# A two-layer graph network on one core: 93 of 3126 gathers of 128 rows replaced by single-row DMAs from SyncE and ScalarE

## The reference, cut to what matters

```python
h = x @ W
norm = dinv[src] * dinv[dst]
msgs = h[src] * norm[:, None]
out = jax.ops.segment_sum(msgs, dst, num_segments=n)
return out + b
```

## Time and profile before

| | us |
|---|---|
| median of 3 runs | 4136.05 |
| fastest, slowest run | 4133.31, 4149.07 |
| span of the profiled execution, first to last instruction | 4132.4 |
| POOL busy in it | 3025.7 |
| PE busy in it | 3066.6 |
| DVE, ACT busy in it | 1279.2, 392.7 |

### The profile page before, as it was taken

How to read it: one execution, slowest core, us unless ns; L and a number is a source line. 1 busy time by engine, 2 the same in 40 slices (tenths; PEclk the granted TensorE clock), 3 DMA queues, 4 the chain that set the end, 5 groups by cost and what they waited for, 6 DMA issues and landing times.

```text
span 4132.4 us, 36624 instructions
## 1 busy us (share of the span) xinstructions
PE 3066.6 (74%) x12107; PEld 1945.3 (47%) x12107; DVE 1279.2 (31%) x2593; ACT 392.7 (10%) x1088; POOL 3025.7 (73%) x3173
## 2 busy tenths in 40 slices
PE   6677777777776777777777777777778877777778
PEld 6344444443443443344444554444445555555556
DVE  8222222222222222222222233332224444434456
ACT  7000000000000000000001111111111111111112
POOL 3677777777777777777767777777777777777773
PEclk9878888888889888888879889999998899999988
DMA  8444444444444444444434444443334444444455
GB/s 268 135 118 118 118 119 119 118 119 120 119 118 119 118 121 118 119 119 118 121 100 119 119 118 121 118 118 112 113 113 120 117 118 118 115 121 129 118 153 176
DMA packets 248738, 513.99 MB, mean 124 GB/s; under 512 B 62491, under 2 KB 141832, under 8 KB 248296
## 3 DMA queue, kind: packets, MB, share of 16 engines
q0 software_dynamic: 150048, 410.73, 35.6%
q1 hardware_dynamic: 98504, 100.82, 8.2%
HBM read 471.70 MB, written 39.64 MB: 124 GB/s over the span
## 4 chain that ended last, share of the span: by engine, by line
POOL 66%; issue 22%; DMA 5%; PE 4%; DVE 1%; ACT 1%; SPq 0%; POOLq 0%; DVEq 0%
POOL sb_big L956 66%; DMA sb_big<-T,sb_srci 4%; PE bank L1241 2%; PE bank L570 1%; PE bank L1728 0%; ACT sb_big L791 0%; PE bank L1703 0%; PE bank L1713 0%; DVE sb_big L857 0%; DMA T<-sb_big 0%; PE bank L550 0%; DVE sb_big L859 0%; DMA sb_work<-dstT 0%; POOL sb_X L1900 0%; DVE sb_looks L668 0%
## 5 line engine op out<-in xcount | busy, mean ns | idle before, releaser
L956 POOL DMA_INDIRECT sb_big<-T,sb_srci x3126 | 2960.4, 947 | 975.9 <-issue 943.3
L1241 PE MATMUL bank<-sb_big 128*128 (+2 forms) x7056 | 2511.2, 463 | 987.8 <-DMA sb_big<-T,sb_srci 938.1
L1241 PEld LDWEIGHTS bank<-sb_big 128*128 128x128 f32 x7056 | 1303.3, 216 | 1954.6 <-issue 1816.3
L1001 DVE SCALAR_TENSOR_TENSOR sb_big<-sb_dstf,bank 128x2304 f32<-128x2304 f32 x196 | 499.0, 2546 | 29.9 <-issue 29.8
L1031 DVE SCALAR_TENSOR_TENSOR sb_work<-sb_bW,sb_work,bank 128x256 f32<-128x256 f32 x98 | 47.2, 481 | 1292.3 <-PE bank L1168 1292.3
L1016 DVE TENSOR_TENSOR sb_work<-bank,sb_work 128x257 f32<-128x257 f32 (+1 forms) x196 | 83.2, 425 | 461.3 <-PE bank L1241 461.3
L1040 DVE SCALAR_TENSOR_TENSOR sb_work<-bank,sb_dinv,sb_b 128x256 f32<-128x256 f32 x98 | 47.4, 484 | 529.3 <-PE bank L1168 529.3
L1070 ACT COPY sb_work<-bank 128x256 f32<-128x256 f32 x196 | 73.0, 373 | 1263.9 <-PE bank L1129 1263.9
L1050 DVE TENSOR_TENSOR sb_X<-sb_X,bank 128x256 f32<-128x256 f32 x98 | 41.2, 421 | 390.2 <-PE bank L1181 390.2
L1079 ACT ACTIVATE sb_work<-sb_work,sb_dinv 128x256 f32<-128x256 f32 x98 | 49.9, 509 | 878.4 <-DVE sb_work L1032 878.4
L1128 PE MATMUL bank<-sb_ident,sb_work 128*128 128x128 f32 x392 | 118.7, 303 | 16.9 <-DVE sb_work L1040 11.9
(11 more groups left out here) (200 smaller groups left out, 1719.7 us busy)
## 6 DMA issues: line engine op xcount, KB each, us to landing
sb_big<-T,sb_srci POOLq DMA_INDIRECT x3126, 2.8
sb_work<-T SPq DMA_DIRECT2D x49, 257.0 KB
T<-sb_work SPq DMA_DIRECT2D x49, 256.0 KB, 2.4
sb_work<-T SPq DMA_DIRECT2D x49, 256.0 KB
sb_X<-x SPq DMA_DIRECT2D x13, 896.0 KB, 11.1
out<-sb_X SPq DMA_DIRECT2D x9, 1024.0 KB
T<-sb_big SPq DMA_DIRECT2D x8, 899.5 KB, 6.0
sb_looks<-LO SPq DMA_DIRECT2D x23, 256.0 KB
```

The source lines that it names most:

```text
L956: pool.indirect_dma_start(out, None, table, bass.IndirectOffsetOnAxis(idx, 0)).then_inc(s.g[u % NSEM], 16)
L1001: v.scalar_tensor_tensor(t.S[:, b * K:(b + 1) * K, :], t.dstf[:, bass.ds(tj, K)].unsqueeze(2).to_broadcast([P, K, P]), float(-P * j), psum ...
L1241: mm = pe.matmul(ps.A[b][:, 0:w], t.S[:, b * K + k, :], rhs, start=(k == 0), stop=(k == K - 1))
```

## The change

93 chunks, 55 in convolution 1 and 38 in convolution 2, are left out of POOL's sequence. They are called lane chunks: about every 27th chunk in convolution 1 and about every 35th in convolution 2, none in the last tiles. Each of their 128 rows is fetched by a DMA of its own, 1028 or 1024 bytes, into one of 4 new slots (`lane`). SP issues 75 of the rows of a chunk and ACT 53 in convolution 1, 93 and 35 in convolution 2 (`ROW_RATES`), at up to 45 and 32 rows a tile, then 42 and 16. The issuing engine reads the row offsets into its registers, up to 32 by one load, from two small lists that are loaded and scaled at the start (`dve_offsets`). When all rows are in, ACT copies the lane slot into the ring (`act_lane`) and PE waits for this copy instead of a gather (`chunk_wait`). The ring has 40 slots instead of 44. ACT also takes over the loads of own rows, the T2 stores and the XT stores.

```diff
-RING = 44
+RING = 40
+LANES = 4
+ROW_RATES = ((75, 53, (45, 32), 24), (93, 35, (42, 16), 24))
+ACT_PARTS = ((16, 16), (0, 16, 0))
+LAST_COPY = (94, 87)
+REGS_A_LOAD = 32
...
+def lane_rows(eng, t, s, a, which, c, j, part=None):
+
+    table, w = ((a.T1, TW), (a.T2, D))[c]
+    flat = table.rearrange("n d -> (n d)").bitcast(U8)
+    todo = LANE_STEPS[2 * c + which][j]
+    if part is not None:
+        todo = todo[sum(ACT_PARTS[c][:part]):sum(ACT_PARTS[c][:part + 1])]
+    while todo:
+        n, p = todo[0]
+        m = next((k for k, (q, _) in enumerate(todo) if q != n), len(todo))
+        m = min(m, REGS_A_LOAD)
+        u = n + len(LANE_CHUNKS[0]) * c
+        if u >= LANES:
+            eng.wait_ge(s.copied, u - LANES + 1)
+        regs = [eng.alloc_register(f"lane{which}_{c}_{n}_{p + k}") for k in range(m)]
+        eng.reg_load(regs, t.offsets[c][LIST0 + n:LIST0 + n + 1, p:p + m])
+        for k in range(m):
+            at = eng.snap(regs[k], donate=True, min_val=0, max_val=4 * w * (N - 1))
+            eng.dma_start(t.lane[p + k:p + k + 1, u % LANES, 0:w].bitcast(U8),
+                          flat[bass.ds(at, 4 * w)].unsqueeze(0)).then_inc(s.rows[c][u % LANES], 16)
+        todo = todo[m:]
+
+
+def act_lane(act, t, s, i):
...
+            act.wait_ge(s.rows[c][u % LANES], 16 * P * (u // LANES + 1 - first))
+            act.wait_ge(s.agg, released(c * ET + e - RING))
+            act.copy(t.ring[:, (c * ET + e + OFF) % RING, 0:w], t.lane[:, u % LANES, 0:w]).then_inc(s.copied, 1)
...
 def pool_conv(pool, t, s, a, c):
...
     for u in range(c * ET, (c + 1) * ET):
+        if u in LANE_OF:
+            continue
...
-            gather_wait(pe, s, c * ET + seen)
+            chunk_wait(pe, s, c * ET + seen)
...
-def act_fast(act, t, s, ps):
+def act_fast(act, t, s, ps, a):
     for i in range(NT):
         act_sum(act, t, s, ps, i, True)
+        lane_rows(act, t, s, a, 1, 0, i, 0)
+        act_own(act, t, s, a, i)
         act_hidden(act, t, s, ps, i, True)
-    act_fast2(act, t, s, ps)
+        lane_rows(act, t, s, a, 1, 0, i, 1)
+        act_store(act, t, s, a, i)
+    act_fast2(act, t, s, ps, a)
...
+def sp_fast1(sp, t, s, a):
+    load_own(sp, t, s, a.T1, TW, 0)
+    sp_low(sp, t, s, a)
+    sp.wait_ge(s.scaled, 2)
+    for j in range(NT):
+        lane_rows(sp, t, s, a, 0, 0, j)
+
+
+def sp_fast2(sp, t, s, a):
+    load_own(sp, t, s, a.T2, D, 0)
+    for j in range(NT):
...
+        if any(n % 2 and ROWS[row_of(n)][0] == n for n, ph, q in SLOTS.get(j + 2, [])):
+            sp.wait_ge(s.Y, NT + j + 1)
+        sp_looks(sp, t, s, a, j + 2)
+        lane_rows(sp, t, s, a, 0, 1, j)
```

More of the change, by code:

```diff
@@ L217, in views @@
     work = sb("work", [P, WORK])
-    t.ring, _ = take(big, 0, [RING, TW])
-    t.ring3, _ = take(big, 0, [RING * TW // XW, XW])
-    t.S, _ = take(big, RING * TW, [2 * K, P])
+    t.lane, o = take(big, 0, [LANES, TW])
+    t.ring, _ = take(big, o, [RING, TW])
+    t.slots, _ = take(big, 0, [SLOTS_ALL, TW])
+    t.ring3, _ = take(big, 0, [SLOTS_ALL * TW // XW, XW])
+    t.S, _ = take(big, SLOTS_ALL * TW, [2 * K, P])
     o = 0
@@ L232, in views @@
     t.OH = [v, u] * (NOH // 2 - 1) + [v, w]
-    assert last <= STAGE_SLOT[2] * TW and (STAGE_SLOT[2] + GROUP) * TW <= RING * TW - SPILL
+    assert last <= STAGE_SLOT[2] * TW and (STAGE_SLOT[2] + GROUP) * TW <= SLOTS_ALL * TW - SPILL
     t.bpx, _ = take(looks, 0, [2 * P])
-    assert o <= RING * TW - SPILL, o
+    assert o <= SLOTS_ALL * TW - SPILL, o
     t.loi = t.srci[:, :].rearrange("p (t i) -> p t i", t=2)
@@ L306, in views @@
     t.stage = [staged[:, k, :].rearrange("p (j d) -> p j d", d=TW) for k in range(2)]
-    t.stage += [t.ring[:, k:k + GROUP, :] for k in STAGE_SLOT[2:]]
+    t.stage += [t.slots[:, k:k + GROUP, :] for k in STAGE_SLOT[2:]]
     o = 0
@@ L322, in views @@
     t.lowb, o = take(looks, o, [2, P], BF16)
+    scaled, o = take(looks, o, [P], I32)
+    t.offsets = [scaled, ones[:, :].bitcast(I32)]
     t.alf, o = take(t.Wc[:, :, :].rearrange("p c d -> p (c d)"), 0, [NT, 4])
@@ L339, in views @@
     t.prodd, o = take(big, o, [2, 512])
-    assert o <= RING * TW, o
-    t.maskd, o = take(big, RING * TW, [NT * PD])
+    assert o <= SLOTS_ALL * TW, o
+    t.maskd, o = take(big, SLOTS_ALL * TW, [NT * PD])
     t.same32, o = take(big, o, [NT, WIN], BF16)
-    assert o <= RING * TW + K * P
-    t.M, o = take(big, RING * TW + K * P, [4, BATCH * P])
-    assert o <= RING * TW + 2 * K * P
+    assert o <= SLOTS_ALL * TW + K * P
+    t.M, o = take(big, SLOTS_ALL * TW + K * P, [4, BATCH * P])
+    assert o <= SLOTS_ALL * TW + 2 * K * P
     t.MT, o = take(work, 0, [4, BATCH * P])
@@ L466, in semaphores @@
     s.fput = [s.fput0, s.fput1]
+    s.rows = [[s.fg0, s.fg1, s.fcur0, s.fcur1], [sem(f"rows{k}") for k in range(LANES)]]
+    s.copied, s.scaled, s.listed = s.fput0, s.fput1, s.fin
     return s
@@ L969, in released, with lane_tables @@
     return next(n for n, upto in enumerate([0] + READ_UPTO) if upto > u) if u >= 0 else 0
+def lane_tables():
+    lists, steps, copies, e0 = [], [], [], 0
+    for c in range(2):
+        sp, act, per, delta = ROW_RATES[c]
+        rows, at, n = [], [], 0
+        while True:
+            last = max(ceil((n + 1) * sp / per[0]) + LAG, ceil((n + 1) * act / per[1]) + 1 if act else 0)
+            e = P // 8 * (last + 1) + delta
+            if last > LAST_COPY[c]:
+                break
+            rows.append(e)
+            at.append(last)
+            n += 1
+        lists.append(rows)
+        copies.append(at)
+        for eng, (lo, hi) in enumerate(((0, sp), (sp, P))):
+            step = [[] for _ in range(NT)]
+            for r in range(len(rows) * (hi - lo)):
+                step[r // per[eng]].append((r // (hi - lo), lo + r % (hi - lo)))
+            steps.append(step)
+    return lists, steps, copies
@@ new lines, with first_need @@
+LANE_CHUNKS, LANE_STEPS, LANE_COPIES = lane_tables()
+LANE_OF = {c * ET + e: sum(map(len, LANE_CHUNKS[:c])) + n for c in range(2) for n, e in enumerate(LANE_CHUNKS[c])}
+LIST0 = 64
+assert max(map(len, LANE_CHUNKS)) <= min(P - LIST0, 15 * LANES)
+def first_need(c, e):
+    return next((j, k) for j in range(NT) for k in range(K) if min(UB[j] + k, ET - 1) >= e)
+for c, (rows, at) in enumerate(zip(LANE_CHUNKS, LANE_COPIES)):
+    for e, j in zip(rows, at):
+        assert released(c * ET + e - RING) <= NTH * (c * NT + j + 1), (c, e, j)
+        assert first_need(c, e) > (j + 1, PLACE1[0] + 1), (c, e, j, first_need(c, e))
@@ new lines, in landed, with chunk_wait @@
+def landed(u):
+    return 16 * sum(1 for v in range(u % NSEM, u + 1, NSEM) if v not in LANE_OF)
+def chunk_wait(eng, s, u):
+    if u in LANE_OF:
+        eng.wait_ge(s.copied, LANE_OF[u] + 1)
+    else:
+        eng.wait_ge(s.g[u % NSEM], landed(u))
+def lane_rows(eng, t, s, a, which, c, j, part=None):
[18 more added lines that the diff above has]
+        todo = todo[m:]
@@ new lines, in act_lane @@
+def act_lane(act, t, s, i):
+    c, j = divmod(i, NT)
+    w = (TW, D)[c]
+    for e, at in zip(LANE_CHUNKS[c], LANE_COPIES[c]):
+        if at == j:
+            u = LANE_OF[c * ET + e]
+            first = sum(1 for v in range(u % LANES, len(LANE_CHUNKS[0]), LANES)) if c else 0
+            act.wait_ge(s.rows[c][u % LANES], 16 * P * (u // LANES + 1 - first))
+            act.wait_ge(s.agg, released(c * ET + e - RING))
+            act.copy(t.ring[:, (c * ET + e + OFF) % RING, 0:w], t.lane[:, u % LANES, 0:w]).then_inc(s.copied, 1)
@@ L972, in pool_conv, with dve_offsets @@
+def dve_offsets(v, ch, t, s):
+    v.wait_ge(s.listed, 32)
+    for c, w in enumerate((TW, D)):
+        lists = t.offsets[c][LIST0:LIST0 + len(LANE_CHUNKS[c])]
+        v.tensor_scalar(lists, lists, 4 * w, None, ALU.mult).then_inc(s.scaled, 1)
 def pool_conv(pool, t, s, a, c):
@@ L1583, in dve_looks, with load_own, act_own, act_store @@
                                t.red[:, 0:4 * (c1 - c0)].rearrange("p (e h) -> p e h", h=4), ALU.add))
-def sp_node_tiles(sp, t, s, a, c, table, fast):
+def load_own(eng, t, s, table, w, j):
+    rows = table[j * P:(j + 2) * P, :].rearrange("(t p) d -> p t d", p=P)
+    eng.dma_start(t.self[:, :, 0:w], rows).then_inc(s.self, 16)
+def sp_fast1(sp, t, s, a):
[7 more added lines that the diff above has]
+    for j in range(NT):
+        if j in (NT - 3, NT - 2):
+            sp.wait_ge(s.agg, NTH * (NT + j + 1))
+            sp_own_all(sp, t, s, a, j - NT + 3)
+        if any(n % 2 and ROWS[row_of(n)][0] == n for n, ph, q in SLOTS.get(j + 2, [])):
+            sp.wait_ge(s.Y, NT + j + 1)
+        sp_looks(sp, t, s, a, j + 2)
+        lane_rows(sp, t, s, a, 0, 1, j)
+def act_own(act, t, s, a, i):
+    c, j = divmod(i, NT)
+    if j % 2 and j + 1 < NT:
+        act.wait_ge(s.Y, i + 1)
+        load_own(act, t, s, (a.T1, a.T2)[c], (TW, D)[c], j + 1)
+def act_store(act, t, s, a, j):
+    if j % 2:
+        act.wait_ge(s.R, j + 1)
+        two = a.T2[(j - 1) * P:(j + 1) * P, :].rearrange("(t p) d -> p t d", p=P)
```

(15 more changed lines are left out.)

54 lines of the change are left out of this document (37 added, 17 removed).

## The result

The changed kernel takes 4299.0 us (median of 4 runs, 4297.1 to 4304.6) against 4136.7 us before (now the median of 4 runs): a ratio of 1.039, 95% interval 1.037 to 1.041. It is 162 us slower where I forecast 113 us faster. The first views, in the order of the ones before.

A forecast was written before the change was run, and what follows sets the result against it. POOL's gathers, one every 1.25 us, were taken as the bound. The 4132.4 us span less 116.4 for 93 gathers, plus 3 for late copies and lane waits and 3.6 for median over profile, gave 4023 us; range 4010 to 4150.

The forecast's parts named there:

- What bounds the kernel: POOL's gathers set the time: one starts every 1.25 us, 0.95 of gather and 0.30 of pause.
- What the change removes: In POOL's sequence, 93 gathers at 1.2515 us, 116.4 us: 68.8 in convolution 1, 47.6 in convolution 2.
- PE, DVE, the ring, the moved DMAs: PE and DVE work, 40 slots, and own-row loads and stores on ACT: all hidden, cost nothing.
- the cover: POOL's room in the ring ahead of PE: some 15 chunks, 19 us, before POOL would stop.
- SP's new work: SP's rows at 0.33 us and register loads at 1.1: 17.1 of 19.3 us a tile in convolution 1, cost nothing.
- number 1: SP's rows or register loads make SP the bound, kernel slower; chance 0.13 through rows, 0.03 through loads.
- its second form: SP's register loads grow 0.09 us a register, 4.2 us more a tile, 4326 us; chance 0.03.
- its first: SP's rows cost over 0.38 us each: 4140 us at 0.40, 4530 at 0.45; chance 0.13.
- number 2: SP's and ACT's issues take turns on something shared: 3.0 us a tile over in convolution 1, 4300 us; chance 0.08.
- Number 3: ACT becomes the bound at 20.3 us a tile, 1.0 over, 4115 us; chance counted with number 1.
- number 4: POOL's gathers slow by 0.03 us each because of added packets, taking 91 us back, 4114 us; chance 0.03.
- ACT: ACT's rows, loads, copies and moved DMAs take 15.0 of 19.3 us a tile in convolution 1, cost nothing.

The follow-up runs named there:

- e7_aligned: The changed kernel with same lane chunks and rows, each register load beginning at a multiple of four words, reading up to three unused registers: 4033.9 us, ratio 0.973.
- e5_fours: The changed kernel with row counts in multiples of four, 90 lane chunks, ACT taking up a chunk only when its lane is free: 4034.4 us, ratio 0.973.
- e11_more: e7_aligned with the schedule of e5_fours and more rows, 102 lane chunks instead of 93: 4009.3 us, ratio 0.970.
- e9: The changed kernel with one lane chunk in each convolution; ring of 40, flags, waits and moved DMAs kept: 4135.5 us, ratio 1.000.
- e12_sp_only: e5_fours with only SP issuing rows, all 128 of a chunk, 57 lane chunks: 4065.1 us, one run.
- e8_aligned_sp: e7_aligned with only SP's loads aligned, ACT's left as in the changed kernel: 4036.9 us, ratio 0.973.

## Why the prediction was wrong, step by step

- **What bounds the kernel**: right. POOL's 1.25 us a gather set the time, and the runs with aligned loads return nearly that for each gather taken out: e7_aligned 111 us for 93, 1.20 each, e5_fours 111 us for 90 and e11_more 126 us for 102, 1.23 each.
- **What the change removes**: right in size, 116.4 us; the sum of 4023 us is within 0.3% of the 4034 us that the same rows take once the loads are aligned (4024 us by the ratio of 0.973).
- **PE, DVE, the ring, the moved DMAs**: right that they are hidden (e9). The condition that I named, that POOL stops if PE falls back too far, came true. The size of the cover is not confirmed: in the stall shown above POOL got four gathers further after PE had stopped, not 15. And "PE is held by landing data at nearly every step" was read too high: the trace of before has 1565 such waits for 3126 gathers, one for every second gather.
- **SP's new work**: this is the step that failed, and in it only one of its two prices. The row was taken from `lbub` at 0.33 us and is 0.331. The register load was taken at 1.1 us and is 3.6 on average: 183 of them in convolution 1 take 655 us instead of 201. That is 454 us more against a spare of 2.2 x 92 = 202 us; 252 us over, of which 209 show as lost time in convolution 1, the rest having been slack at the ends that I had not counted. In convolution 2 the 185 loads take 580 us instead of 204, against a spare of 2.5 x 85 = 212 us: 164 over, of which 62 show.
- The failure was in reading. The 7-register row has a minimum of 1058 and a median of 1701 ns. I took this as spread. In the records of before it is two values: the loads for tiles 0, 28, 56 and 84, whose first word is a multiple of four, take 1.06 to 1.09 us, and all the others, which start at words such as 7 or 14, take 1.70 to 1.72. The 16-register row, from which I argued that the number of registers hardly matters, has loads whose first word is a multiple of 16 only. So the argument "16 registers take no longer than 7" compared different cases. That row is no clean measure either: one of its seven loads fetches only 2 registers (98 = 6 x 16 + 2) and takes 1.08 us, and three of the others take 1.39 to 1.72 us where three take 1.11; no run says why.
- The rule that I weighed and set aside, 200 ns for each register ("the Trainium skill", page "Runtime: NRT & Kernel Launch", section "Instruction fetch mechanics"), gives the price of the loads that do not begin at a multiple of four: 32 registers at 6.9 us are 0.21 each. It does not hold for those that do: 2.17 us are 0.07 each. I had counted it 45 x 0.2 = 9 us a tile, in fact SP's loads took 655 / 92 = 7.1 us, since a part of the loads did begin at a multiple of four (43 of the 120 loads of 32 registers in the two convolutions).
- **Rivals**: number 1 is what happened, through its second form (loads that grow with the count, chance 0.03, 4326 us) and not through its first (rows above 0.38 us, 0.13). The place and nearly the time (4299) were in the list with the smallest chance, but the growth with the count was only half of the mechanism, since it hangs on where the load begins. That 4326 lies so near is luck: with the measured loads the same sum gives 4023 + 252 + 164 = 4439 us, and the slack that I left out takes most of the difference back. The 4300 us of number 2 meet the measured time by chance too; it is refuted by e12_sp_only and e7_aligned. Number 3 is refuted by e8_aligned_sp, number 4 by the gathers' 0.946 us, here and in e11_more, which has 13056 row DMAs.
- **ACT**: with the changed kernel's loads it had less room than I gave it, but it still fits (e8).

## What to carry to other kernels

A minimum far below the median in a row of one kind of instruction is a question, not a spread: split it by operand before its median enters a sum, above all where that instruction is to be issued hundreds of times more. When work is moved to an engine that looked idle, its price is the price of everything that must be issued for it, and a budget of 2 us in 19 is decided by the least known term; that term is worth a bound from the worst row, not the usual one. The fix here was free: start each list of offsets that is loaded into registers at a multiple of four words, or read up to three words more than are needed. The trace of e11_more suggests the same for the end of the list: there 19 registers took ACT 1.91 us and 20 took 1.45. A kernel that rounds up both ends was not run.

## What the runs showed of the hardware

- A load into registers of SP or ACT from SBUF costs about 0.21 us a register when its first word is not a multiple of four words (16 bytes) within the partition (32 registers 6.9 us, 16 registers 3.7), and about 0.07 when it is (2.17 and 1.22 us). The same two levels stand in the loads of PE and DVE before the change (7 registers 1.70 and 1.06 us, 1.63 and 1.04 us).
- The 0.07 us holds for counts that are multiples of four. After the last full four, each further register costs about 0.22 us: from a multiple of four on ACT took 1.21, 1.45, 1.66 and 1.89 us for 16, 17, 18 and 19 registers (medians, e7_aligned), and 1.45 us again for 20 (e11_more). How the hardware fetches them is not shown by these runs.
- A one-row DMA of 1028 or 1024 bytes with its address in a register is issued every 0.322 us by SP and every 0.325 by ACT at the median while both issue; SP alone has 0.322 as well (e12_sp_only). ACT alone was not run.
- 11904 such DMAs beside the gathers left the gathers at 0.95 us; to their landing it took 2.9 us at the median in the changed kernel and 3.0 in e7_aligned (2.8 before). The DMA share rose from 0.43 to 0.46 in the stretch of the earlier trace rows in e7_aligned.
